# Cross-attention mask as a product of two 64-row matrices in four row tiles; constants in three packed arrays, first loads issued from two queues

## The reference, cut to what matters

```python
x = x + self_attn(layernorm(x))                # 16 heads of 8
x = x + cross_attn(layernorm(x), ctx, ctx)     # 16 heads of 64, rotary
x = x + ffn(layernorm(x))                      # top-1 of 8 experts, and a shared one

# cross_attn:
qh = rope((q @ wq.T).reshape(b, l, 16, 64)); kh = rope((k @ wk.T).reshape(b, l, 16, 64))
vh = (v @ wv.T).reshape(b, l, 16, 64)
scores = einsum('bhqd,bhkd->bhqk', qh, kh) * 64 ** -0.5
i, j = arange(l)[:, None], arange(l)[None, :]
scores = where((j <= i) & (j >= i - 32), scores, -1e30)     # the mask
out = einsum('bhqk,bhkd->bhqd', softmax(scores), vh) @ wo.T
```

## Time and profile before

| | |
|---|---|
| three runs | 831.12, 832.52, 833.48 us; median 832.52 |
| the profiled execution | 831.49 us, of which 829.7 us is its span |
| busy in the span | PE 778.4 us (94%), DVE 532.4, ACT 536.7, POOL 535.0 (64 or 65% each) |
| mean granted TensorE clock | 0.983 |
| moved by transfers | 64.12 MB, 77 GB/s in the mean |

### The profile page before, as it was taken

One profiled execution on the slowest core, in us unless ns is written; L12 is line 12 of the kernel. 1 busy time (PEld: TensorE's weight loads), 2 busy tenths in 40 slices (PEclk: granted clock), 3 DMA queues, 4 the chain that ended last, 5 costly groups with the idle time before them and its releaser, 6 DMA issues. The chain is left out here.

```text
span 829.7 us, 27387 instructions
## 1 busy us (share of the span) xinstructions
PE 778.4 (94%) x9724; PEld 625.9 (75%) x9724; DVE 532.4 (64%) x1355; ACT 536.7 (65%) x1900; POOL 535.0 (64%) x864
## 2 busy tenths in 40 slices
PE   1789999999999999999999999999899999999894
PEld 1467888888888888888888888888687778777562
DVE  1456666666666666777777776666665856665652
ACT  1357777777777777777777777777666666566352
POOL 4246677677777777766677667777566565765544
PEclk9889999999999999999999999999899999999997
DMA  7031222222222122222222222223131112314230
GB/s 229 7 117 62 81 87 75 79 65 87 73 81 90 62 69 69 69 70 68 69 70 68 69 69 70 69 68 124 58 108 48 44 44 95 97 61 131 69 109 12
DMA packets 58517, 64.12 MB, mean 77 GB/s; under 512 B 5231, under 2 KB 54901, under 8 KB 58385
## 3 DMA queue, kind: packets, MB, share of 16 engines
q1 hardware_dynamic: 55376, 55.80, 21.1%
q0 software_dynamic: 3008, 6.57, 2.3%
HBM read 17.91 MB, written 45.35 MB: 76 GB/s over the span
## 5 line engine op out<-in xcount | busy, mean ns | idle before, releaser
L802 ACT ACTIVATE PX<-P,mx 128x128 f32<-128x128 f32 x512 | 183.0, 407 | 85.2 <-DVE mx L565 85.2
L565 DVE TENSOR_REDUCE mx<-P 128x4 f32<-128x512 f32 x128 | 83.1, 673 | 172.7 <-PE P L302 172.7
L965 POOL TENSOR_TENSOR PX<-PX,mx 128x512 f32<-128x512 f32 x128 | 133.0, 1040 | 16.5 <-DVE mx L570 16.5
L802 ACT ACTIVATION_READ_ACCUMULATOR PX<-P,mx 128x1 f32 x512 | 127.0, 248 | 0.0
L960 POOL TENSOR_TENSOR rq<-rq,tq 128x1024 f32<-128x1024 f32 x32 | 75.5, 2359 | 60.6 <-DVE rq L529 60.6
L504 DVE TENSOR_REDUCE nmf<-P 128x4 f32<-128x512 f32 x128 | 81.3, 678 | 9.0 <-PE P L203 6.9
L766 ACT ACTIVATE PS<-P 128x512 f32<-128x512 f32 x128 | 70.7, 609 | 23.8 <-PE P L224 23.8
L811 ACT ACTIVATE PT<-P 128x512 f32<-128x512 f32 x128 | 76.4, 597 | 8.3 <-PE P L311 5.9
L311 PE MATMUL P<-ident,PX 128*128 128x128 f32 x512 | 79.3, 278 | 0.0
L311 PEld LDWEIGHTS P<-ident,PX 128*128 128x128 f32 x512 | 57.4, 142 | 24.1 <-issue 22.7
L955 POOL TENSOR_TENSOR rk<-rk,tk 128x1024 f32<-128x1024 f32 x32 | 75.2, 2350 | 0.0
(11 more groups left out here) (145 smaller groups left out, 1783.1 us busy)
## 6 DMA issues: line engine op xcount, KB each, us to landing
z_xs<-fill SPq DMA_DIRECT2D x34, 1088.0 KB, 5.4
xrow<-z_xs SPq DMA_DIRECT2D x46, 136.0 KB, 2.3
ew<-in_ew SPq DMA_DIRECT2D x9, 384.0 KB, 3.9
x<-in_x SPq DMA_DIRECT2D x32, 64.0 KB, 1.8
cxT<-in_ctxT SPq DMA_DIRECT2D x32, 64.0 KB, 1.8
out<-yst,xrow POOLq DMA_INDIRECT x46, 2.3
wk<-in_wk SPq DMA_DIRECT2D x1, 512.0 KB, 3.6
tab<-in_tab SPq DMA_DIRECT2D x1, 512.0 KB, 5.1
```

What stands on the lines that cost most here:

```text
L565: dve.tensor_reduce(mx[b % 3][:, 0, r, :], v3(bank(f"ds{r}")), AX.X, ALU.max, negate=True).then_inc(S["v_dm"][r], 1)
L802: t = act.activation(PX[(4 * b + r) % 6][:, c, :], p[:, c * 128:c * 128 + 128], ACT.Exp, bias=m[:, 0, r, c:c + 1], scale=1.0, accum_out=m[ ...
L965: pool.tensor_tensor(X[:, :, :], X[:, :, :], mx[b % 3][:, 2, r, :].rearrange("p (h a) -> p h a", a=1).to_broadcast([128, 4, 128]), ALU.mul ...
```

## The change

The mask is factored. 63 sets of queries are formed: 58 sets of queries that stand 58 apart, and 5 sets of up to 26 neighbours. Row k of `rows` is 1 at the queries of set k; row k of `cols` is 0 at the keys that any query of the set may see, and -1e30 elsewhere. The sum over k of `rows[k, q] * cols[k, j]` is 0 where query q may see key j and -1e30 or twice that elsewhere. The 64 rows (one is empty) are held as two halves h of 32, each repeated on all four groups of 32 partitions, in bfloat16. `d_s` now has eight mask matmuls of 32 rows by 512 moving columns, h outside and r inside:

```diff
-                for r in range(4):
-                    pe.matmul(v3(p[r]), identb[:, :],
-                              mask[:, :].rearrange("p (a k) -> p a k", a=1).to_broadcast([128, 4, 128]),
-                              start=True, stop=False, skip_group_check=True)
+                for h in range(2):
+                    for r in range(4):
+                        pe.matmul(v3(p[r]), rows[32 * r:32 * r + 32, h, :],
+                                  cols[32 * r:32 * r + 32, h, :].rearrange("p (a k) -> p a k", a=1).to_broadcast([32, 4, 128]),
+                                  start=(h == 0), stop=False, skip_group_check=True)
```

The constants are packed into three arrays: `c1` (128 x 646 float32: identity, projection weights, biases, a selector), `cb` (128 x 1296 values of 16 bits: the bfloat16 ones, already in that type, with `rows` and `cols`), `c2` (128 x 712 float32: the rest). The casts on DVE go, and with them its waits. ACT issues five loads and SP eleven, 16 in all:

```diff
-            dve.wait_ge(S["d_c"], 16 * NC1)
-            dve.tensor_copy(identb[:, :], ident[:, :]).then_inc(S["v_const"], 1)
-            dve.wait_ge(S["d_c2"], 16 * NC2)
-            dve.tensor_copy(mask[:, :], stage[:, 0, :]).then_inc(S["v_const"], 1)
...
+            act.dma_start(c1[:, :], A["c1"]).then_inc(S["d_c1"], 16)
+            act.dma_start(cxT[0][:, :], A["ctxT"][0]).then_inc(S["d_cx"][0], 16)
+            act.dma_start(cb[:, :], A["cb"]).then_inc(S["d_cb"], 16)
+            act.dma_start(tab[:, :, :, :].rearrange("p w e t -> p (w e t)"), A["tab"]).then_inc(S["d_tab"], 16)
+            act.dma_start(c2[:, :], A["c2"]).then_inc(S["d_c2"], 16)
             act.wait_ge(S["p_init"], 1)
             act.activation(warm[:, :], nhalf[:, :], ACT.Exp)
-            act.wait_ge(S["d_c"], 16 * NC1)
...
             load_x(0)
-            for dst, src in ((ident, "ident"), (winT, "winT"), (bqk, "bqk"), (bv, "bvb"), (bo, "bob"), (jm, "jm")):
-                sp.dma_start(dst[:, :], A[src]).then_inc(S["d_c"], 16)
+            sp.dma_start(wk[:, :, :, :].rearrange("p e c n -> p (e c n)"), A["wk"]).then_inc(S["d_wk"], 16)
             load_x(1)
...
+            sp.dma_start(wvT[:, :, :].rearrange("p t n -> p (t n)"), A["wvT"]).then_inc(S["d_wv"], 16)
+            load_cx(1)
+            sp.dma_start(wq[:, :, :, :].rearrange("p e c n -> p (e c n)"), A["wq"]).then_inc(S["d_wq"], 16)
             load_x(2)
+            load_cx(2)
+            sp.dma_start(woT[:, :, :].rearrange("p t n -> p (t n)"), A["woT"]).then_inc(S["d_wo"], 16)
+            sp.dma_start(ew[:, NE, :], A["ew"][:, EW * NE:EW * NE + EW]).then_inc(S["d_we"], 16)
+            load_cx(3)
```

More of the change, by code:

```diff
@@ L8 @@
 U32 = mybir.dt.uint32
+U16 = mybir.dt.uint16
 ALU = mybir.AluOpType
@@ L26 @@
 EW = 768
+MOST = 36
+C2 = 640 + 2 * MOST
 BANKS = dict(xt=1, xg=3, xr=2, xy=2)
@@ L33 @@
 S0, PERIODS = 24, 42
[L34 to L38 removed]
+SEMS = """d_c1 d_cb d_c2 d_wk d_wv d_wq d_wo d_we d_ex d_tab
+p_init p_own v_own
 t_a s_aT t_qkv s_q v_km v_v
@@ L63, in build @@
         P = ctx.enter_context(nc.psum_tensor("P", [128, 8, 512], F32))
-        ident = sb("ident", [128, 128])
-        identb = sb("identb", [128, 128], BF16)
+        c1 = sb("c1", [128, 646])
+        cb = sb("cb", [128, 1296], U16)
+        c2 = sb("c2", [128, C2])
         tab = sb("tab", [128, 4, 2, 128])
-        mask = sb("mask", [128, 128], BF16)
-        upper = sb("upper", [128, 128], BF16)
         ones = sb("ones", [128, 128], BF16)
[L71 to L79, removed]
         nhalf = sb("nhalf", [128, 1])
         warm = sb("warm", [128, 1])
[L82 to L86, removed]
         wq = sb("wq", [128, 2, 4, 128])
@@ L141, in build @@
         yst = ring("yst", 4, [128, 128])
-        stage = ew[:, 0:2, :].rearrange("p a (b n) -> p (a b) n", n=128)
+        ident, winT, bv = c1[:, 0:128], c1[:, 128:512], c1[:, 512:640]
+        bqk, jm = c1[:, 640:642], c1[:, 642:646]
+        identb, upper = cb[:, 0:128].bitcast(BF16), cb[:, 128:256].bitcast(BF16)
+        sel = cb[:, 256:768].bitcast(BF16).rearrange("p (j k) -> p j k", j=4)
+        ecap = cb[:, 768:784].bitcast(BF16).rearrange("p (c e) -> p c e", c=2)
+        rows, cols = (cb[:, 784 + 256 * k:1040 + 256 * k].bitcast(BF16).rearrange("p (h n) -> p h n", h=2) for k in range(2))
+        woutT, bo, fill, tri = c2[:, 0:128], c2[:, 128:256], c2[:, 256:256 + ROW], c2[:, 528:592]
+        tri = tri.rearrange("p (a b) -> p a b", a=8)
+        rtT, iota, ids = c2[:, 592:600], c2[:, 600:608], c2[:, 608:640].bitcast(U32)
+        steps, tiles = c2[:, 640:640 + MOST], c2[:, 640 + MOST:640 + 2 * MOST]
         ewf = ew[:, 0:NE, :].rearrange("p e n -> p (e n)")
@@ L1156 @@
     i, j = np.arange(128)[:, None], np.arange(128)[None, :]
-    band = np.where((j <= i) & (j >= i - 32), f(0), f(-1e30)).astype(f)
     w = {n: np.asarray(inputs[n]) for n in _INS}
@@ L1179 @@
     choose = np.where((part < 3)[:, None] & (head[:, None] == np.arange(4)), f(1), f(0)).astype(f)
-    arrays["stage"] = np.concatenate([band, np.triu(np.ones((128, 128), f), 1), np.repeat(choose, 128, axis=1),
-                                      np.pad(np.concatenate([np.arange(8, dtype=f) * f(128 * n) for n in CHUNKS])[None],
-                                             ((0, 127), (0, 112)))], axis=1)
-    arrays["jm"] = (row[:, None] % 32 // 8 == np.arange(4)).astype(f)
-    arrays["ids"] = (np.arange(32)[None, :] * 128 + row[:, None]).astype(np.uint32)
@@ L1185 @@
-    arrays["fill"] = np.zeros((128, ROW), f)
-    arrays["fill"][:, ID] = (4096 + row).astype(np.uint32).view(f)
-    arrays["tiles"] = np.tile(np.arange(32, dtype=f), (128, 1))
-    arrays["iota"] = np.tile(np.arange(8, dtype=f), (128, 1))
-    arrays["steps"] = np.tile(np.arange(32, dtype=f) * f(128), (128, 1))
-    arrays["tri"] = np.tile(np.tril(np.ones((8, 8), f)).reshape(1, 64), (128, 1))
-    arrays["bqk"] = w["L0_attn_b_in"][0:256].reshape(2, 128).T
-    arrays["bvb"] = np.ascontiguousarray(np.broadcast_to(w["L0_attn_b_in"][256:384], (128, 128)))
@@ L1193 @@
-    arrays["bob"] = np.ascontiguousarray(np.broadcast_to(w["L0_attn_b_out"], (128, 128)))
+    every = lambda a: np.broadcast_to(np.asarray(a, f).reshape(1, -1), (128, np.size(a)))
+    bits = lambda a: np.asarray(a, np.uint32).view(f)
+    eye, b_in = np.eye(128, dtype=f), w["L0_attn_b_in"]
+    near = lambda q: (j <= q) & (j >= q - 32)
+    sets = [row[r::58] for r in range(58)] + [row[26 * r:26 * r + 26] for r in range(5)]
+    rows, cols = np.zeros((2, 64, 128), f)
+    for k, q in enumerate(sets):
+        rows[k, q], cols[k] = 1, np.where(near(q[:, None]).any(axis=0), f(0), f(-1e30))
@@ new lines @@
+    four = lambda a: np.tile(a.reshape(2, 32, 128).transpose(1, 0, 2).reshape(32, 256), (4, 1))
+    half = np.concatenate([eye, np.triu(np.ones((128, 128), f), 1), np.repeat(choose, 128, axis=1),
+                           every([np.arange(8) * 128 * n for n in CHUNKS]) * (row[:, None] == 0),
+                           four(rows), four(cols)], axis=1).astype(f)
+    arrays["cb"] = (half.view(np.uint32) >> 16).astype(np.uint16)
+    arrays["c1"] = np.concatenate([eye, win.T, every(b_in[256:384]), b_in[0:256].reshape(2, 128).T,
+                                   row[:, None] % 32 // 8 == np.arange(4)], axis=1).astype(f)
@@ L1195 @@
+    fill = np.zeros((128, ROW), f)
+    fill[:, ID] = bits(4096 + row)
+    arrays["c2"] = np.concatenate([w["L0_attn_w_out"].T, every(w["L0_attn_b_out"]), fill, every(np.tril(np.ones((8, 8)))),
+                                   w["L0_ffn_router"].T, every(np.arange(8)), bits(np.arange(32)[None, :] * 128 + row[:, None]),
+                                   every(np.arange(MOST) * 128), every(np.arange(MOST))], axis=1)
     arrays = {n: np.ascontiguousarray(a) for n, a in arrays.items()}
```

54 lines of the change are left out of this document (13 added, 41 removed).

## The result

| | before | after |
|---|---|---|
| median of the runs | 833.0 us (831.12 to 834.26, 4 runs) | 806.98 us (806.54 to 811.08, 4 runs) |
| the profiled execution | 831.49, span 829.7 | 806.58, span 804.8 |
| mean granted TensorE clock | 0.983 | 0.984 |

The ratio is 0.970, with a 95% interval of 0.9671 to 0.9729: 26 us less, where 809 was predicted. The same kernel, run again beside later experiments, had a ratio of 0.9693 (0.9678 to 0.9707).

The account below looks back on a forecast made before the run. PE was taken as the bound in the steady state. From the profiled 831.5, 16.7 (mask) and 6.5 (start) came off: 808.3; the median runs 1.0 higher, so 809 was predicted, range 801 to 822.

Parts of the forecast that it names:

- The mask's step: On PE in `d_s`, mask's start to scores' start: 0.43 us instead of 0.97, saving 0.54 us a batch.
- The estimate from the Trainium skill's 3.07 times: Eight mask matmuls at 0.57 us, saving 0.40 a batch, result some 4 us higher; the sum did not use it.
- The scores' first round: First four score matmuls behind the mask: some 0.1 us of weight loading could be hidden, making the most saving 0.64.
- the mask's term: Mask matmuls over 31 batches: 31 x 0.54 = 16.7 us saved, ends 9.6 and 19.8.
- The start's term: Filling of the pipeline: 7 us left of 9.8, less half a microsecond for the clock, 6.5; ends 3 and 10.
- Does it reach the end: After `d_s` on PE: no input comes late when 0.54 us goes; `f_pos` is tightest with 0.4 us to spare.
- Rival B: The mask's gain turns into a wait on PE: half kept gives 818, nothing kept 826; chance 0.12.
- The start: Before the first maxima: PE's first transpose near 6.2, `x(3)` landed by 15, DVE's first maxima at 16.7 instead of 23.70.
- Rival A: The start is bound by bytes, not issue: first maxima gain only 2.5 us, 813; chance 0.13.
- Rival D: The eight mask matmuls don't overlap: 1.76 us, 0.79 more than before, giving 850; chance 0.04.

Follow-up runs that it names:

- experiment 4: The changed kernel with each half of the mask added twice, 16 mask matmuls instead of eight: 821.87 us, ratio 0.9849.
- experiment 1: The changed kernel's constants and loads, but the mask again as four full-array matmuls of an identity by the mask: 826.35 us, ratio 0.9909.
- experiment 3: The changed kernel with the eight mask matmuls left out, the scores starting the accumulation: 799.76 us, ratio 0.9578.
- Experiment 9: The changed kernel run again, unaltered, as a control: 806.98 us, ratio 0.9693 to the kernel before.
- experiment 6: The changed kernel with x(0) to x(2) first on SP and the three loads needed last issued behind x(3) and x(4): 800.49 us, ratio 0.9664.
- experiment 2: The changed kernel with the eight mask matmuls in the other order, r outside and h inside: 807.98 us, ratio 0.9703.
- experiment 5: The changed kernel with all 16 first loads issued by SP, the two lists interleaved: 806.0 us, ratio 0.9723.
- experiment 7: The changed kernel with 42 idle matmuls of ones on PE where it waits in the first 50 us: 800.29 us, ratio 0.9649.
- experiment 8: The kernel before with its 14 small constant loads issued by ACT instead of SP: 833.61 us, ratio 1.0051.

## Why the prediction was right, step by step

- **The mask's step.** Predicted 0.43 us, measured 0.44. That four row groups stream at once at full speed was read from line 224's rounds of 0.05 us; experiment 4 gives 0.22 us for each round of 512 columns. The estimate from the Trainium skill's 3.07 times (page TensorE: Matmul & The Clock Gate, section Measured speedup vs the span model), 0.57 us, is not what happens here.
- **The scores' first round.** The prediction named 0.1 us for it and left it out of the middle value. It is there, 0.12 (1.88 for 2.00), in every batch, and experiments 1, 3 and 4 show that what stands in front decides: 2.00 behind a full-array mask or behind `d_pv`, 1.88 behind row tiles. So the saving in an ordinary period was 0.62 and not 0.54; 31 x 0.08 would be 2.5 us more. But it didn't all arrive. In the profiled executions the mask's term is 0.5 us (batch 0) + 14.5 + 2.1 = 17.1, against 16.7 predicted: a few longer periods, and those with expert tiles, kept the rest. The start's term is 9.1 - 0.5 = 8.6, against 6.5, and the end took 0.8. Together that is 24.9, where 23.2 was predicted against that execution (831.5 to 808.3); in the medians it is 26.0 against 23.5. So the mask's sum came out right with two errors that nearly cancel, which is in part luck, and most of what was missing is the start's.
- **Does it reach the end.** Yes: PE 99.8% busy, period 0.62 shorter. `f_pos` had 0.26 us to spare in the period shown, where 0.4 was worked out. Rival B is out: experiment 4's 0.44 a period is the full price.
- **The start.** First transpose 6.39 (near 6.2 predicted), `x(3)` at 14.8 (15), first maxima 16.37 (16.7). `x(0)` landed at 3.85 and not at 2.6; POOL's memsets hid all but 0.25 us of that. The start as a whole gave 8.2 us by experiment 1 (834.53 - 826.35; its interval is 6.0 to 9.3), where 6.5 was taken. Its profiled execution has the second mask group at 65.83, only 5.8 us earlier than before, where the changed kernel's gained 8.6 without the mask's part. Of these 2.8 us, 1.75 lie in the first scores: they took 3.70 us in the one and 1.95 in the other, because a slow stretch fell on them or didn't. So the 6.5 lies within what the runs show, and most of what went beyond it in the execution shown is where the clock fell. It isn't less slow time in all: from 20 to 60 us the mean granted clock was 0.83 before and after. Experiment 9, the same kernel with 3.16 us for these scores, shows that this part changes from run to run.
- **The tail** gave back 0.8 us in the profiled execution. It was in no step. Whether it is a cost of the change isn't shown: with the same code there it took from 83.9 to 87.5 us in the later profiles (experiments 6 and 2).
- **Rival A** (bytes, not issue) has a share of truth: experiments 5 and 6 show DVE waiting for bytes in the queue. But these came at 392 GB/s in the mean from 4 to 14 us in the changed kernel, and the first maxima still moved up by 7.3 us. **Rival D** is refuted by the 0.44.

## What to carry to other kernels

When one engine is busy all the time, count its work from start to start and look for a place in the same trace where the new form already runs: sixteen small matmuls told the price of eight large ones to 0.01 us. Look also at the seams: a group behind one of the same array shape loads its first weights unseen, which was worth a fifth of the mask's gain here (0.12 of 0.62 us a batch). And at the start, who waits for what mattered more than how many queues issue (4.4 us of the first maxima against 1.6). Splitting the queues alone made the old kernel slower by half a per cent; the small loads that everything waits for then landed later, most likely because they shared the transfer engines with big ones that nobody needed yet.

## What was not expected of the hardware

- Two matmuls on one row group, issued together, don't hold up those on other row groups: eight took 0.44 us in either order (experiment 2).
- The 32-row float32 scores' group took 2.00 us behind a group of another array shape (experiments 1 and 3) and 1.88 behind 32-row tiles (the changed kernel and experiment 4): its first round costs 0.12 us more behind another shape.
- Idle matmuls of ones in the gaps took away both stretches at a granted clock of 0.50 (1.2 GHz) after 20 us, together some 13 us long (10 us at a mean of 0.51, 4 at 0.57); by themselves they gave 2.35 us at the second mask group; in the time of the whole kernel the intervals don't separate their gain from none (experiment 7).
- 14 loads of constants, moved to a second queue, were issued sooner, and the last landed 3.5 us later (experiment 8).
